# Three score banks and two maxima banks in both attention stages of a one-core transformer kernel

## The reference

```python
def _L1_xattn_ref(query, key, value, attn_mask, Wq, Wk, Wv, Wo):     # cross stage
    q, k, v = _heads(query @ Wq.T), _heads(key @ Wk.T), _heads(value @ Wv.T)
    logits = einsum('bhqd,bhkd->bhqk', q, k) * SCALE
    masked = where(mask, logits, -1000000000.0)
    weights = softmax(masked, axis=-1) * mask
    weights = weights / maximum(weights.sum(-1, keepdims=True), 1e-09)
    return merge(einsum('bhqk,bhkd->bhqd', weights, v)) @ Wo.T

def _attention(x, Wq, bq, Wk, bk, Wv, bv, Wo, bo):                   # self stage
    q, k, v = heads(x @ Wq + bq), heads(x @ Wk + bk), heads(x @ Wv + bv)
    attn = softmax(einsum('bqhd,bkhd->bhqk', q, k) / sqrt(dh), axis=-1)
    return merge(einsum('bhqk,bhkd->bqhd', attn, v)) @ Wo + bo

x = x + aft(layernorm(x), ctx)                    # L0
x = x + moe_expert_choice(layernorm(x))           # L0
x = x + _L1_xattn_ref(layernorm(x), ctx, ctx, mask, ...)
x = layer1_self_attention_and_moe(x)              # L1, router and experts behind the self attention
```

## Time and profile before

| | us |
|---|---|
| median of 3 runs | 2768.06 |
| lowest, highest | 2766.54, 2769.54 |
| the profiled execution, its own time | 2763.92 |
| its span, first to last instruction | 2762.1 |
| mean granted TensorE clock | 0.907 |
| cross stage: first maximum, first score, last score | 678.0, 699.6, 1331.9 |
| self stage: first maximum, first score, last score | 1398.1, 1419.1, 2010.0 |

### The profile page before, as it was taken

The page is one execution under the profiler, slowest core; times in us unless marked ns, Lnnn a source line. Parts: engine busy times, 40 slices in busy tenths (PEclk is TensorE's granted clock), DMA queues, the critical chain, the costliest instruction groups (busy, mean ns, idle before and its releaser), DMA issues. The chain is left out here.

```text
span 2762.1 us, 39121 instructions
## 1 busy us (share of the span) xinstructions
PE 2310.8 (84%) x10904; PEld 1292.4 (47%) x10904; DVE 1339.5 (48%) x3501; ACT 1020.2 (37%) x1827; POOL 739.6 (27%) x764
## 2 busy tenths in 40 slices
PE   6694169994999999999589999999937999999991
PEld 2463146661343333443223333333316888888880
DVE  3555643313666666666257776777644111111115
ACT  2230012110455555556226555555611222232232
POOL 0110023334221022220142233332211333333335
PEclk9885579995999999999779999999967999999995
DMA  4310044426233244231043334323203666666654
GB/s 142 101 61 30 0 126 98 115 55 131 38 49 49 39 55 55 36 44 25 22 56 46 47 56 55 51 37 47 40 8 116 179 193 181 183 185 180 194 149 131
DMA packets 196359, 235.27 MB, mean 85 GB/s; under 512 B 21538, under 2 KB 177698, under 8 KB 195682
## 3 DMA queue, kind: packets, MB, share of 16 engines
q1 hardware_dynamic: 174498, 202.90, 32.0%
q0 software_dynamic: 21696, 30.42, 6.1%
HBM read 146.23 MB, written 35.91 MB: 66 GB/s over the span
## 5 line engine op out<-in xcount | busy, mean ns | idle before, releaser
L1728 DVE CUSTOM_DVE_ANT_0 atL1x_junk<-atL1x_pm,bias 128x512 bf16<-128x512 f32 x512 | 346.0, 688 | 228.7 <-PE atL1x_pm L1408 226.7
L1724 DVE TENSOR_REDUCE atL_tops<-atL_pm 128x1 f32<-128x512 f32 x512 | 339.7, 684 | 175.2 <-PE atL_pm L1408 169.3
L1565 ACT ACTIVATE atL1x_prob<-atL1x_ps 128x512 f32<-128x512 f32 x512 | 303.7, 598 | 288.5 <-PE atL1x_ps L1425 279.8
L1027 PE MATMUL exL_po<-exL_w,exL_hid 128*128 128x256 f32 x1760 | 393.2, 382 | 16.6 <-DVE exL_ys L1092 8.6
L1011 PE MATMUL exL_ph<-exL_xgT,exL_w 128*128 128x256 f32 (+1 forms) x1504 | 399.3, 421 | 6.0 <-ACT exL_hid L1043 3.6
L1565 ACT ACTIVATE atL_prob<-atL_ps 128x512 f32<-128x512 f32 x512 | 294.8, 599 | 254.3 <-PE atL_ps L1422 251.4
L1027 PEld LDWEIGHTS exL_po<-exL_w,exL_hid 128*128 128x128 f32 x1760 | 330.0, 190 | 71.1 <-issue 16.7
L1043 ACT ACTIVATE exL_hid<-exL_ph,exL_b 128x256 f32<-128x256 f32 (+1 forms) x376 | 190.1, 511 | 433.3 <-PE exL_ph L1011 412.2
L1011 PEld LDWEIGHTS exL_ph<-exL_xgT,exL_w 128*128 128x128 f32 x1504 | 276.8, 192 | 112.9 <-issue 59.6
L977 POOL DMA_INDIRECT sum<-exL_ys,exL_put x110 | 180.1, 1637 | 424.3 <-DVE exL_ys L1092 243.2
L1422 PE MATMUL atL_ps<-atL_qstack,atL_kstack 99*128 99x512 bf16 x512 | 201.5, 396 | 16.4 <-DMA atL_qstack<-atL_negT 5.8
(11 more groups left out here) (328 smaller groups left out, 2750.0 us busy)
## 6 DMA issues: line engine op xcount, KB each, us to landing
exL_w<-in_L_W SPq DMA_DIRECT2D x94, 1024.0 KB, 4.9
atL1x_kstack<-atL1x_k SPq DMA_DIRECT2D x96, 128.0 KB, 4.6
atL1x_qstack<-atL1x_q SPq DMA_DIRECT2D x96, 128.0 KB, 6.4
atL_kstack<-atL_k SPq DMA_DIRECT2D x96, 128.0 KB, 4.6
atL_qstack<-atL_q SPq DMA_DIRECT2D x96, 128.0 KB, 6.6
exL_b<-in_L_b SPq DMA_DIRECT2D x47, 128.0 KB, 5.4
sum<-tok_zero SPq DMA_DIRECT2D x1, 4224.0 KB, 15.5
aft_ctxT<-in_ctxT SPq DMA_DIRECT2D x2, 2048.0 KB, 10.1
```

The lines of the kernel that those rows point to most:

```text
L1027: mm = pe.matmul(po[c % 2][:], hid[:, f, c * P:(c + 1) * P], w2[slot][:, f, :], start=f == 0, stop=f == FC - 1)
L1565: act.activation(prob[i % PROBS][:], ps[i % 2][:], ACT.Exp, scale=SCALE).then_inc(s["p_ready"], 1)
L1724: ins = dve.tensor_reduce(tops[g % 2][:, t, j:j + 1], pm[i % TOPS][:], AX.X, ALU.max)
L1728: ins = dve.tensor_tensor_reduce(junk[:, i % TOPS, :], pm[i % TOPS][:], G["bias"][0][:, t, :], 1.0, -BIG / 2, ALU.add, ALU.max, tops[g % 2 ...
```

## The change

The bank counts are exchanged: maxima have two banks (`TOPS` = 2), scores three (`SCORES` = 3). A score may now start when the exponential three back is done, a maximum when the reduction two back is done. The rule for a batch's first steps, which `tops_before` stated for the maxima, is now used for both, as `bank_before`. The cross stage's `junk`, an unread output of L1728, has as many slices as there are maxima banks, so two. Below the constant every line number is one higher.

```diff
-TOPS = 3
+TOPS = 2
+SCORES = 3
...
-        ps = [st.ps(f"ps{i}", [P, S]) for i in range(2)]
+        ps = [st.ps(f"ps{i}", [P, S]) for i in range(SCORES)]
...
-        def tops_before(i):
-
-            if i >= TOPS:
-                return i - TOPS + 1
-            return max(k for k in range(PER) if k % TOPS == i) + 1 - PER
+        def bank_before(i, banks):
+
+            if i >= banks:
+                return i - banks + 1
+            return max(k for k in range(PER) if k % banks == i) + 1 - PER
...
-                        pe.wait_ge(s["m_done"], past(b * PER + tops_before(i)))
+                        pe.wait_ge(s["m_done"], past(b * PER + bank_before(i, TOPS)))
...
-                    if not (isinstance(b, int) and b == 0 and i < 2):
-                        pe.wait_ge(s["p_ready"], past(b * PER + i - 1))
-                    mm = pe.matmul(ps[i % 2][:], stack["k"][par][0:KR + 3, h, kc * P:(kc + 1) * P],
+                    if not (isinstance(b, int) and b == 0 and i < SCORES):
+                        pe.wait_ge(s["p_ready"], past(b * PER + bank_before(i, SCORES)))
+                    mm = pe.matmul(ps[i % SCORES][:], stack["k"][par][0:KR + 3, h, kc * P:(kc + 1) * P],
...
-                            act.activation(prob[i % PROBS][:], ps[i % 2][:], ACT.Exp, scale=SCALE).then_inc(s["p_ready"], 1)
+                            act.activation(prob[i % PROBS][:], ps[i % SCORES][:], ACT.Exp, scale=SCALE).then_inc(s["p_ready"], 1)
```

More of the change, by code:

```diff
@@ L1419, in score_step @@
                         pe.wait_ge(s["neg_in"], past((b * NG + g + 1) * 16))
-                    if not (isinstance(b, int) and b == 0 and i < 2):
-                        pe.wait_ge(s["p_ready"], past(b * PER + i - 1))
-                    mm = pe.matmul(ps[i % 2][:], stack["k"][par][0:KR + 3, h, kc * P:(kc + 1) * P],
+                    if not (isinstance(b, int) and b == 0 and i < SCORES):
+                        pe.wait_ge(s["p_ready"], past(b * PER + bank_before(i, SCORES)))
+                    mm = pe.matmul(ps[i % SCORES][:], stack["k"][par][0:KR + 3, h, kc * P:(kc + 1) * P],
                                    stack["q"][par][0:KR + 3, h, :], start=True, stop=self_)
                     if not self_:
-                        mm = pe.matmul(ps[i % 2][:], G["identb"][:], G["bias"][1][:, kc, :], start=False, stop=True)
+                        mm = pe.matmul(ps[i % SCORES][:], G["identb"][:], G["bias"][1][:, kc, :], start=False, stop=True)
                     mm.then_inc(s["s_ps"], 1)
```

## The result

The changed kernel took 2775.41 us in the median of 20 runs, the kernel before 2768.34 us in the median of 20: a ratio of 1.0034 with a 95% interval of 1.0019 to 1.0048 (the quotient of the two medians is 1.0026). The time lies inside the forecast range of 2762 to 2780, 4.9 us above the forecast of 2770.5. By the ratio it is slower by more than 0.2%, though the low end of the interval, 1.0019, just reaches into that band; so the case that I held likeliest (within 0.2%, 0.55) did not come, and the one behind it (slower, 0.32) did. The profiled execution of the changed kernel took 2771.86 us with a span of 2770.02, against a span of 2762.09 before: 7.9 us more.

A forecast was written before the change was run, and what follows sets the result against it. TensorE was taken to bound both attention stages, with bank counts mattering where it meets a full bank. Terms gave -0.6 us cross and +3.0 self, together +2.4 on 2768.06, so 2770.5 us; range 2762 to 2780.

The forecast's parts named there:

- Term 1: Lead-in of both stages: with two banks a maximum takes 0.76 us instead of 0.61; +3.9 us cross, +3.5 self.
- Terms 2 and 3: Cross stage's batch boundaries: maxima no longer wait for the bank just used, -5.0 us; first scores now do, +2.9 us.
- Term 4: Last batch's second half: a third bank spares scores waits for exponentials; -2.4 us cross stage, -1.4 self stage.
- Term 5: Self stage's loop: maxima wait instead of scores; near zero over seven batches (-3 to +5), last batch's first half +0.9.
- the walk: Self stage, one batch followed step by step: +0.2 in a clean block, about +0.9 or +0.2 us over a batch.
- the cover at the batch's end: Self stage's batch boundary: the next first score's DMA wait, 1.94 us, hides the batch's loss; -0.45 on three batches.
- Slower because nothing is hidden: Rival: self-stage loop waits add up instead of ending in the DMA's wait; 7 x 1.9 = 13 us more, 2784; chance 0.1.
- Slower by the clock: Rival: new waits behind the self stage's router jobs bring two more half-clock stretches, 8.5 us, 2779; chance 0.2.
- The rival's own sign: Slower by the clock decides if half-clock stretches come in four or more batches of the self stage.
- Faster: Rival: the lead-in keeps its pace and two half-clock stretches do not return, 2756; either alone 2762 to 2764; chance 0.13.
- does nothing: Rival: terms cancel exactly, or TensorE has slack at each place; 2768 us, chance 0.1.
- The rule of the Trainium skill: Whole kernel: both kernels use all eight PSUM banks, so the change's sum would be nothing and the time 2768.1 us.

The follow-up runs named there:

- the second trace of before: The kernel before, unchanged, traced once more; the self stage's seven batches took 533.7 us with 23.9 us at half clock.
- the self stage alone: Against the kernel before, maxima two and scores three banks in the self stage only, cross stage kept at three and two; ratio 1.0048, median 2780.4 us.
- the borrowed bank: The changed kernel, but each stage's lead-in maxima go over three banks, the third an idle scores' bank; ratio to the kernel before 1.0025, median 2772.2 us.
- the third trace: The changed kernel, unchanged, traced a third time; the self stage's seven batches took 541.6 us with 37.5 us at half clock.
- two and two: The changed kernel with two banks for maxima and two for scores in both stages, one bank unused; ratio to the kernel before 1.0048.
- the mended scores' wrap: The changed kernel, but a batch's last score takes the second score bank, except in the last batch; ratio to the kernel before 1.0039.
- the shared bank: The changed kernel, but maxima have the fifth bank in the lead-in and steps 44 to 63, scores otherwise; ratio to the kernel before 0.9981, median 2760.8 us.
- the second trace: The changed kernel, unchanged, run and traced again; ratio to the kernel before 1.0051, median 2781.0 us.
- the mended kernel: The kernel before, with a batch's last maximum on the second bank and the last batch's scores from step 33 over five banks; ratio 0.9951, again 0.9970.

## Why the prediction was right in its range and wrong in its likeliest case

**Term 1, the lead-in: right.** Forecast +3.9 and +3.5, measured +4.4 and +3.4 in each of three traces. The self stage's +3.4 holds 0.2 us of clock: its first maxima ran at full clock in the trace of before (21.02) and at half clock in the changed kernel's (24.40). Like with like it is +3.2 (24.40 against 21.22 in the second trace of before, both at half clock) or +3.0 (23.97 in the self stage alone against 21.02). The 0.5 us taken off for an earlier return of full clock did not come. The maximum's pace of 0.76 us (0.695 in the self stage) and its cause (a bank too few, not VectorE) are shown by the borrowed bank.

**Terms 2 and 3, the wraps: right.** Forecast -5.0 and +2.9 in the cross stage, -2.1 together. Measured -2.0 over the six batches whose clock was the same; batch 5 is at -1.7, but before it had 3.4 us at half clock that the first trace lacks, and in the third trace it is at +1.1. Mended alone, the maxima's wrap is worth 0.66 to 0.75 us a batch and the scores' 0.58 to 0.72.

**Term 4, the last batch's second half: right in the cross stage, too small in the self stage.** Forecast -2.4 and -1.4, measured -2.5 and -2.5. For a self-stage block I took 0.28 us; the measured gain is 2.5 over five blocks, 0.5 each. It is due to the third score bank: two and two has 0.0.

**Term 5, the self stage's loop: here the prediction failed.** Forecast near zero for seven batches (-3 to +5); measured +4.6 between two traces that both have 30.7 us at half clock, and more in the traces that have more of it. Inside a batch the walk was right. In the clean block the scores no longer wait and the maxima do:

```profile
1543.19 0.38 PE L1423 MATMUL atL_ps<-atL_qstack,atL_kstack 99*128 99x512 bf16 x1
1543.70 0.39 PE L1409 MATMUL atL_pm<-atL_kstack,atL_qstack 96*128 96x512 bf16 x1
1543.92 0.38 PE L1423 MATMUL atL_ps<-atL_qstack,atL_kstack 99*128 99x512 bf16 x1
1544.30 0.39 PE L1409 MATMUL atL_pm<-atL_kstack,atL_qstack 96*128 96x512 bf16 x1
1544.62 0.64 PE L1441 MATMUL atL_po<-atL_prob,atL_vals 128*32 128x512 f32 x4
```

From the block's first score (1542.31) to its value matmuls it takes 2.31 us, against 2.10 before (1540.29 to 1542.39): the forecast's 0.2. At the end of batch 1 step 62 stands 1.37 us later than before (+0.9 forecast). The step that failed is the cover at the batch's end. I had put -0.45 on a batch that ends in the DMA's wait; at the first score of batch 2 it is +0.05. Part of the difference, 0.3 us by the mended scores' wrap, is that this score is no longer released by the DMA but by ScalarE, whose exponential of step 63 has the same bank. And I ended the walk at that first score, where another +0.7 us comes behind it. The changed kernel at this boundary, TensorE and then VectorE:

```profile
1562.53 0.39 PE L1409 MATMUL atL_pm<-atL_kstack,atL_qstack 96*128 96x512 bf16 x1 [1.00 <-DVE atL_tops L1725]
...
1565.50 0.38 PE L1423 MATMUL atL_ps<-atL_qstack,atL_kstack 99*128 99x512 bf16 x1 [0.61 <-ACT atL_prob L1566]
...
1566.88 0.39 PE L1409 MATMUL atL_pm<-atL_kstack,atL_qstack 96*128 96x512 bf16 x1 [0.57 <-DVE atL_tops L1725]
...
1561.78 1.89 DVE L1725 TENSOR_REDUCE atL_tops<-atL_pm 128x1 f32<-128x512 f32 x3 [0.23 <-DVE atL_rshift L1787]
1564.49 0.69 DVE L1725 TENSOR_REDUCE atL_tops<-atL_pm 128x1 f32<-128x512 f32 x1 [0.83 <-PE atL_pm L1409]
```

The last maximum of the block waits 1.00 us for VectorE (1562.53). Value matmuls and the next score come behind it in TensorE's order, so VectorE in turn gets nothing and idles 0.83 us (1564.49). It is late from then on, and when the first score has been released, the second maximum of the new batch waits for it again (1566.88). The 1.94 us of DMA wait in the earlier trace rows covered TensorE's loss, but nothing covered VectorE's: in the trace of before its four reductions ran without a break over that point. That the first score's own release is not what counts is shown by the mended scores' wrap: there the score stands 0.3 us earlier, and step 12 stands where it did. With the shared bank the DMA's wait is back, at the corresponding first score of batch 4:

```profile
1712.48 0.39 PE L1461 MATMUL atL_ps<-atL_qstack,atL_kstack 99*128 99x512 bf16 x1 [1.69 <-DMA atL_qstack<-atL_negT]
```

The term by its pieces at full clock: +1.0 at each of three boundaries inside the loop's body, +1.2 behind batch 0 and behind batch 6, together +5.4; the middle of a batch -0.19 six times and -0.33 once, -1.5; so +3.9. The two boundaries at the loop's return (behind batches 2 and 4) are left: no trace of the new counts shows them at full clock. The two traces at equal half clock give +4.6. The first half of the last batch, +1.4, was put at +0.9.

**The rivals.** "Slower because nothing is hidden" named the right place (VectorE behind at the batch's start) with a price of 1.9 a batch; 1.0 to 1.2 came. "Slower by the clock" came too: on one chip the mean clock was 0.0051 lower over 8 runs of the changed kernel than over 22 of the one before. Within the 20 runs first shown 0.001 of mean clock goes with 1.9 us (fitted; they reach from 2764.4 us at 0.909 to 2793.1 at 0.896). An estimate from these numbers: the 0.0051 are worth 9.7 us, and the 8 runs are 14.4 us slower in the mean, which leaves 4.7 for the places; the pieces at equal clock give about +5.8, without the two boundaries at the loop's return. For the 20 runs first shown there is no such split, since the clock of the runs of before that were measured with them is not on record. The rival's own sign, stretches at the ends of four or more batches of the self stage, is met in the second trace (batches 3 to 6) and not in the first (two) or the third (three). Its price per stretch was too high: 0.5 us per us of half clock, where pairs of traces give 0.22 to 0.45, and 1.9 us per 0.001 of mean clock, which is 5.6 us at half clock of a run of 2775, gives 0.34. "Faster" and "does nothing" fell. The rule of the Trainium skill (Perfetto Trace Analysis, Matmul Optimizations) that all eight PSUM banks be in use did not tell these kernels apart: the changed kernel uses all and is slower, two and two leaves one idle, and at the self stage's boundaries the two take the same 33.3 to 33.4 us.

**Sum.** Forecast +2.4; the stages of the first trace +5.0 (cross -1.9, self +6.9), the rest of its 7.9 outside of them, where the second trace has +8.9 and the third -0.3 with no work changed. What stays open is why the clock falls more often under the new counts. TensorE is somewhat less busy over a boundary (28.77 of 33.33 us against 28.33 of 32.36), but no experiment changed that alone, so it stays a guess. It is also open why the kernels with a mended wrap, and the one with the borrowed bank, show half clock behind both of the cross stage's loop returns (3.4 or 6.8 us each), and the kernel before only behind one (3.4 us).

## What to carry to other kernels

Walk a wait past the point where TensorE is released, on both engines: a wait that is hidden for the waiting engine may have starved its partner, whose delay comes back as the next wait. In this kernel the third buffer was worth most to the reader that has other work between its reads, at the time when it has it (VectorE at a batch's end), and it need not belong to it all the time: lending a bank in the lead-in, in the last batch and at a batch's end was worth more than the choice of counts (ratios to the kernel before of 0.998 with the new counts and a shared bank, 1.003 to 1.005 without), and the two small edits of the mended kernel (an uneven wrap, idle banks for the tail) gave 0.3 to 0.5%. Where the clock moves by itself, compare pieces of the trace that ran at one clock, and take the clock from many runs.

## What the runs showed of the hardware that I had not expected

The seven batches of the self stage, one row a trace (columns as in the windows above). The changed kernel:

```profile
1420.50:1960.30 539.80, 504.08 (x2573) 199.50 (x2572) 385.39 (x846) 306.02 (x561) 173.96 (x163) 0.96 0.36 49
```

the changed kernel again:

```profile
1425.60:1974.00 548.40, 515.07 (x2574) 202.22 (x2572) 385.54 (x846) 307.12 (x561) 174.00 (x163) 0.94 0.36 48
```

The same instructions and the same VectorE work, 8.6 us apart: a spread of one stage between executions that is larger than the whole effect of the change. Such a stage cannot be compared from one trace of each kernel. At full clock, in contrast, the boundary piece repeats to 0.05 us over twelve occurrences in five kernels with two banks for maxima (33.32 to 33.37), so that a difference of 1.0 us in it is beyond doubt from a single trace.
